# The second edge gather of a graph and expert kernel: waits and signals by quad, a lead of 11 pairs

## The chip, the cores and the metric

The kernel runs on one core of one Trainium2 chip. Its engines are TensorE (PE), VectorE (DVE), ScalarE (ACT), GpSimd (POOL) and SyncE (SP), each with a queue of its own. They meet through semaphores only. The metric is the device time of one execution in microseconds, the median of several runs.

## The reference

A graph step is followed by a layer of experts. The change touches the graph step: for each of 100,000 edges, sorted by target node, the normalised row of one end is scaled by the edge's weight and summed into the other end's row; the sums are multiplied by W and added to x.

```python
x.shape == (6250, 256); src, dst, edge_weight: 100000
h    = _layernorm(x) @ W.T
msgs = edge_weight[:, None] * h[dst]
x    = x + segment_sum(msgs, src, 6250)
...
x    = x + experts(_layernorm(x))    # 16 experts, the two best of each row, then a norm
```

The kernel sums the rows before it multiplies by W, which gives the same.

## The kernel before

The 6250 nodes are 49 windows of 128. Edges are first sorted by window into tiles of 128 edges. A first part of them (four tiles a window) is gathered and summed early, in straight code, while the sorting still runs. The rest, up to 640 tiles here, is the second gather. It runs after the tables are ready, in loops, and it is the only stage that the change touches.

Its unit is the pair, two tiles of 128 edges. Two pairs are a quad. 16 pairs are one turn of the ring `hbuf` (PR = 16), and there are 20 turns. For a quad of a window PE runs four matmuls of 128 x 128 by 128 x 256 (fp32, each two rows in the profile), which add into the window's bank: the weights are `picks`, a matrix for each tile that says which edge goes to which node, with the edge's weight in it, and the moving rows are those gathered in `hbuf`. The last quad of a window may hold edges of the next one too, so it is read twice: once as the window's closing quad, and again as the first loop quad of the next window. `picks` is 256 wide for that reason, and its two halves serve even and odd windows.

Five queues take part, in an order written out by hand.

- POOL (`gather_gpsimd`, L464) issues two indirect DMAs for a pair (L473). Ahead of a pair it waits for `used`, the count of pairs that PE has finished: pair p may be issued when all but the last AHEAD = 6 pairs before and with it are used. The row numbers lie in `ix`, copied there by DVE in halves (`number`, L422). POOL waits for `ix_set` at each half turn.
- DVE (`gather_vector`, L481) makes the picks of a pair with two instructions (L498), into one of two buffers. So it waits until the pair before the last one is used. It adds to `pick_ready`. Three times in the stage it also ranks the experts for windows that are done (`choose`).
- SP (`gather_sync`, L444) joins the two: for each pair it waits for `pick_ready` and for the gathered rows (`xn_gathered`), then adds one to `pair_in` (L461).
- PE (`gather_tensor`, L550) waits for `pair_in` ahead of each pair of a quad (L554), and its last matmul of each pair adds one to `used` (L591). The closing quad adds nothing to `used`; its last matmul adds one to `closed`. Behind the closing quad stand, for earlier windows, `turn` (two transposes of the sums of the window before, L565) and `project` (the product with W, the gate's columns and the addition of x for the window before that, L572 to L574). The next window starts with a matmul that puts the first sums into its bank (L588).
- ACT (`gather_scalar`, L612) copies the bank to `agg` when `closed` says so (L634), copies the transposed sums (L616), and takes x and its squares (L621 to L628).

When all windows are through, the experts follow. They need every row, so the end of the second gather delays all that comes after.

## Time and profile before

| | |
|---|---|
| median of 3 runs | 2196.22 us (2194.57 to 2212.91) |
| profiled execution | 2194.18 us, span 2192.4 us |
| PE busy | 1521.2 us, 69% |
| POOL busy | 1206.6 us, 55% |
| DVE busy | 976.2 us, 45% |
| ACT busy | 642.5 us, 29% |
| gathers of the second stage (L473) | 640, first at 604.7 us, last at 1593.2 us |
| granted TensorE clock, mean over the span | 0.831 of full speed |

Busy time is the time in which an engine ran instructions that work on data; waits, register work and the issue of DMAs by queues don't count. "Idle before" a group is the time that the engine stood still ahead of its instructions, and the name behind the arrow is what ended it: an instruction of another engine, a DMA, "issue" where the profile shows no reason, or "remote" where a semaphore moved and the profile can't name who moved it. The granted clock is 0.5 or 1.0 at each moment, 1.2 or 2.4 GHz. The ends of matmuls in the rows are modelled, the times of semaphores are not.

### The profile page before, as it was taken

Reading aid. Unit: us, or ns where it says so; the run is one execution under the profiler, and the core shown is the slowest. Engines: PE = TensorE matmul, PEld = TensorE weight load, DVE = VectorE, ACT = ScalarE, POOL = GpSimd, SP = SyncE. Lnnn points to the kernel's source line nnn. Section 1 sums busy time; section 2 is a strip of 40 time slices with the busy share of each in tenths; the row PEclk is TensorE's granted clock in tenths of the full one; section 3 lists DMA queues with packets and bytes.
Section 4 is the critical chain, followed back from the end, with each engine's and each line's share of the span. In section 5 each row is a group of like instructions: output and inputs, shape, how many; then the busy total and the mean of one; then the engine's idle time right before and its main releaser. Section 6 shows DMA issues by size and latency. Waiting matters only on the chain. (4 is left out here: it accounts for less than half of the span.)

```text
span 2192.4 us, 33976 instructions
## 1 busy us (share of the span) xinstructions
PE 1521.2 (69%) x7875; PEld 1191.4 (54%) x7876; DVE 976.2 (45%) x2548; ACT 642.5 (29%) x1788; POOL 1206.6 (55%) x1170
## 2 busy tenths in 40 slices
PE   6165977775655766666666577766436999998975
PEld 4164766553334544444444344544325998897864
DVE  6997898863322222222222422223164333333348
ACT  5661266641000111110110111011053444443455
POOL 0025658776666666666666656665532555554435
PEclk9596679886678878887888788887659999999988
DMA  5122322223633223222222222222363223225356
GB/s 169 51 71 61 90 60 69 64 74 98 211 105 92 83 83 87 87 86 82 85 86 86 82 77 85 88 85 78 76 155 135 69 71 104 86 81 180 104 166 230
DMA packets 121466, 215.63 MB, mean 98 GB/s; under 512 B 21000, under 2 KB 82755, under 8 KB 121280
## 3 DMA queue, kind: packets, MB, share of 16 engines
q0 software_dynamic: 52864, 140.45, 21.9%
q1 hardware_dynamic: 53664, 56.14, 7.8%
q10 hardware_dynamic: 14880, 18.35, 2.6%
q8 instruction: 26, 0.43, 0.1%
q14 instruction: 32, 0.26, 0.0%
HBM read 172.32 MB, written 42.54 MB: 98 GB/s over the span
## 5 line engine op out<-in xcount | busy, mean ns | idle before, releaser
L473 POOL DMA_INDIRECT hbuf<-xn_rows,ix x640 | 618.3, 966 | 375.1 <-issue 173.2
L556 PE MATMUL bank<-hbuf,picks 128*128 x1640 | 536.2, 473 | 340.6 <-SPq L461 193.7
L556 PEld LDWEIGHTS bank<-hbuf,picks 128*128 128x128 f32 x1640 | 351.2, 232 | 519.0 <-issue 470.9
L498 DVE TENSOR_SCALAR picks<-iota_two,marks 128x256 f32<-128x256 f32 x640 | 247.9, 434 | 726.3 <-remote 420.6
L744 POOL DMA_INDIRECT fbuf<-xn_rows,first_tables x196 | 235.8, 1203 | 122.6 <-PE bank L1269 54.7
L634 ACT ACTIVATE agg<-bank 128x256 f32<-128x256 f32 x49 | 18.8, 383 | 763.3 <-remote 579.3
L1853 PE MATMUL bank<-rowsT,w_sb 128*128 128x128 f32 x1744 | 215.8, 277 | 18.9 <-issue 18.9
L1853 PEld LDWEIGHTS bank<-rowsT,w_sb 128*128 128x128 f32 x1744 | 211.6, 193 | 31.1 <-issue 26.6
L1789 POOL DMA_INDIRECT expert_out<-y_sb,to_i x112 | 111.1, 992 | 189.9 <-DVE y_sb L1898 185.4
L1863 PE MATMUL bank<-w_sb,hT 128*128 128x256 f32 x872 | 207.7, 381 | 0.6 <-ACT hT L1811 0.4
L1287 PE MATMUL bank<-work 128*128 128x192 bf16 x1568 | 161.0, 261 | 62.7 <-DVE work L1075 50.3
L1269 PE MATMUL bank<-fbuf,x 128*128 128x256 f32 x392 | 153.1, 506 | 53.0 <-DMA fbuf<-xn_rows,first_tables 40.6
L1287 PEld LDWEIGHTS bank<-work 128*128 128x128 bf16 x1568 | 143.4, 102 | 85.3 <-issue 80.9
L1811 ACT ACTIVATE hT<-bank,b_cols 128x128 f32<-128x128 f32 x436 | 138.5, 365 | 161.2 <-PE bank L1853 150.8
L1863 PEld LDWEIGHTS bank<-w_sb,hT 128*128 128x128 f32 x872 | 157.0, 190 | 18.9 <-ACT hT L1811 1.6
L733 POOL DMA_INDIRECT edge_groups<-recs,dest_i x56 | 79.1, 1413 | 156.9 <-DVE recs L1082 140.3
L1779 POOL DMA_INDIRECT xt<-xn_rows,from_i x116 | 112.6, 970 | 68.6 <-issue 36.7
L1269 PEld LDWEIGHTS bank<-fbuf,x 128*128 128x128 f32 x392 | 81.0, 241 | 85.1 <-issue 55.8
L1898 DVE TENSOR_TENSOR y_sb<-bank,b_b 128x256 f32 x109 | 46.3, 425 | 163.4 <-PE bank L1863 157.3
L1103 DVE TENSOR_SCALAR x<-iota_two,first_tables 128x128 f32<-128x128 f32 x196 | 64.8, 364 | 107.3 <-PE bank L1269 48.6
L1075 DVE TENSOR_TENSOR work<-work,tables 128x768 bf16<-128x768 bf16 (+2 forms) x176 | 95.5, 599 | 5.6
L1059 DVE TENSOR_TENSOR work<-iota_rows,low_i 128x512 bf16<-128x512 bf16 (+2 forms) x136 | 95.1, 749 | 0.2 <-DVE tables L1154 0.2
(294 smaller groups left out, 1721.7 us busy)
## 6 DMA issues: line engine op xcount, KB each, us to landing
w_sb<-in_L_ffn_w_dram ACTq DMA_DIRECT2D x28, 512.0 KB
hbuf<-xn_rows,ix POOLq DMA_INDIRECT x640
first_sums<-x SPq DMA_DIRECT2D x49, 128.0 KB
first_sums_back<-first_sums SPq DMA_DIRECT2D x7, 896.0 KB
xn_rows<-xn SPq DMA_DIRECT2D x7, 896.0 KB, 4.6
x<-in_x_dram SPq DMA_DIRECT2D x6, 896.0 KB
ya<-expert_out SPq DMA_DIRECT2D x5, 896.0 KB, 5.6
yb<-expert_out SPq DMA_DIRECT2D x5, 896.0 KB, 7.5
```

The source lines that it names most:

```text
L473: pool.indirect_dma_start(hbuf[:, 1 + j, k, :], None, xn_dram, bass.IndirectOffsetOnAxis(ap=ix[:, 2 * j + k:2 * j + k + 1], axis=0)).then_ ...
L498: s = v.tensor_scalar(picks[:, j % 2, k, :], iota_two[:], marks[:, 0, 2 * j + k:2 * j + k + 1], marks[:, 1, 2 * j + k:2 * j + k + 1], ALU. ...
L556: m = nc.tensor.matmul(bk[q][:, 0:D], picks[:, j, k, q * P:(q + 1) * P], hbuf[:, ds(place + j, 1), k, :].rearrange("p s d -> p (s d)"), st ...
L744: pool.indirect_dma_start(fbuf[:, s % RH, :], None, xn_dram, bass.IndirectOffsetOnAxis(ap=fdst_i[:, s:s + 1], axis=0)).then_inc(xn_gathere ...
L1075: s = v.tensor_tensor(fields[n % RM][:, h0:h1, :, :, :], colhot[n % RJ][:, h0:h1, None, :, :].to_broadcast(shape), pieces[:, e0 + h0:e0 + ...
L1269: nc.tensor.matmul(bk[w % 2][:, 0:D], fpicks[:, used % RK, :], fbuf[:, used % RH, :], start=t == 0, stop=t == FT - 1).then_inc(first_used, 1)
L1287: s = nc.tensor.matmul(sums_at[c % 2][h][:, 0:2 * PIECES * SP_], rowhot[n % RP][:, k // 2, h * P:(h + 1) * P, k % 2], fields[n % RM][:, k ...
L1779: pool.indirect_dma_start(xt[:, k, :], None, xn2_dram, bass.IndirectOffsetOnAxis(ap=from_i[:, k:k + 1], axis=0)).then_inc(xt_in[k], 16)
L1789: pool.indirect_dma_start(y_dram, bass.IndirectOffsetOnAxis(ap=to_i[:, k:k + 1], axis=0), y_sb[:, k % 2, :], None).then_inc(y_sent[k], 16)
L1811: act.activation(hT[:, f, :], bk[f][:, 0:P], ACT.Relu, bias=b1_cols[:, ds(e * FB + f, 1)]).then_inc(hT_ready, 1)
L1853: m = nc.tensor.matmul(bk[f][:, 0:P], w1_sb[:, q, b, f * P:(f + 1) * P], rowsT[:, b, :], start=b == 0, stop=b == NB - 1)
L1863: m = nc.tensor.matmul(bk[5][:, 0:D], hT[:, f, :], w2_sb[:, q, f, :], start=f == 0, stop=f == FB - 1)
```

## The change

PE waits once for a quad, for its second pair, and adds two to `used` at its last matmul, in place of one at the end of each pair. POOL's lead AHEAD goes from 6 to 11 pairs. The numbers are copied in quarters of 8 in place of halves of 16, at other points of DVE's turn. In a window of PE, `turn` and `project` stand ahead of the closing quad, behind the loop. DVE's waits for `used`, and SP's and ACT's waits, stay as they are.

```diff
--- before.py
+++ after.py
@@ -386,7 +386,7 @@
 
 
         PR = GR // 2
-        AHEAD = 6
+        AHEAD = 11
         hbuf = sb("hbuf", [P, 1 + PR, 2, D], fp32)
         ix = sb("ix", [P, GR], i32)
         marks = sb("marks", [P, 2, GR], fp32)
@@ -417,10 +417,11 @@
         mean2_set = sem("mean2_set")
         squared2 = sem("squared2")
 
-        HALF = GR // 2
+        PART = PR // 4
+        NUMBERS = 2 * PART
 
         def number(v, i, h):
-            v.tensor_copy(ix[:, h * HALF:(h + 1) * HALF], dst_i[:, ds(i * GR + h * HALF, HALF)]).then_inc(ix_set, 1)
+            v.tensor_copy(ix[:, h * NUMBERS:(h + 1) * NUMBERS], dst_i[:, ds(i * GR + h * NUMBERS, NUMBERS)]).then_inc(ix_set, 1)
 
         assert PR == RH
 
@@ -465,8 +466,8 @@
             pool.wait_ge(tables_ready, FBLK + 1)
             def body(i, ahead):
                 for j in range(PR):
-                    if j % (PR // 2) == 0:
-                        pool.wait_ge(ix_set, i * 2 + (j // (PR // 2) + 1))
+                    if j % PART == 0:
+                        pool.wait_ge(ix_set, i * 4 + (j // PART + 1))
                     await_turn(pool, used, i, PR, j + 1 + PR - ahead)
                     pool.sem_inc(pool_steps, 1)
                     for k in range(2):
@@ -500,12 +501,11 @@
                     s.then_inc(pick_ready, 1)
 
                     if j == 2 and not isinstance(i, int):
-
                         await_turn(dve, pair_in, i, PR, 0)
-                        number(v, i, 1)
-                    if j == PR // 2 + 2:
-                        await_turn(dve, pair_in, i, PR, PR // 2)
-                        number(v, i + 1, 0)
+                        number(v, i, 3)
+                    if j > PART and j % PART == 2:
+                        await_turn(dve, pair_in, i, PR, j - 2)
+                        number(v, i + 1, j // PART - 1)
 
             def choose(w0, w1):
                 n, ws = w1 - w0, slice(w0, w1)
@@ -550,8 +550,8 @@
         def gather_tensor(pe):
             def quad(s, q):
                 place = s & (PR - 1)
+                pe.wait_ge(pair_in, s + 1)
                 for j in range(2):
-                    pe.wait_ge(pair_in, s + j)
                     for k in range(2):
                         m = nc.tensor.matmul(bk[q][:, 0:D], picks[:, j, k, q * P:(q + 1) * P],
                                              hbuf[:, ds(place + j, 1), k, :].rearrange("p s d -> p (s d)"),
@@ -588,15 +588,16 @@
                 nc.tensor.matmul(bk[q][:, 0:D], ident[:], first_sums[:, ds(w, 1), :].rearrange("p w d -> p (w d)"), start=True, stop=False, skip_group_check=True)
                 with pe.Fori(first, end, 2) as s:
                     for m in quad(s, q):
-                        m.then_inc(used, 1)
-
-                for m in quad(end, q):
-                    pass
-                m.then_inc(closed, 1)
+                        pass
+                    m.then_inc(used, 2)
+
                 if not isinstance(w, int) or w >= 1:
                     turn(w - 1, 1 - q)
                 if not isinstance(w, int) or w >= 2:
                     project(w - 2, q)
+                for m in quad(end, q):
+                    pass
+                m.then_inc(closed, 1)
 
             pe.wait_ge(tables_ready, FBLK + TBLK)
             pe.wait_ge(first_summed, NW)
@@ -1192,8 +1193,8 @@
                     dve.wait_ge(recs_turned, FBLK + b + 1)
                     table(b, turned_1(b), min(P, TT - b * P), dst_i, row_f, wgt_f, tables_ready)
                     picks_to(SORT_TILES + 20 + b)
-                number(v, 0, 0)
-                number(v, 0, 1)
+                for h in range(4):
+                    number(v, 0, h)
                 picks_to(FTILES)
                 gather_vector(dve)
```

PE's queue in the loop of one window, before. `pair_in` is SP's count of pairs ready; a matmul here is one tile, L589 is the loop's end:

```order
L556 REGISTER_ALU [waits pair_in]
L556 ISA
L556 MATMUL bank<-hbuf,picks 128x256
L556 ISA
L556 MATMUL bank<-hbuf,picks 128x256
L554 REGISTER_ALU
L556 ISA [waits pair_in]
L556 MATMUL bank<-hbuf,picks 128x256
L556 ISA
L556 MATMUL bank<-hbuf,picks 128x256
L589 REGISTER_ALU
L589 COMPARE_AND_BRANCH
```


The same place in the changed kernel:

```order
L556 REGISTER_ALU [waits pair_in]
L556 ISA
L556 MATMUL bank<-hbuf,picks 128x256
L556 ISA
L556 MATMUL bank<-hbuf,picks 128x256
L556 ISA
L556 MATMUL bank<-hbuf,picks 128x256
L556 ISA
L556 MATMUL bank<-hbuf,picks 128x256
L589 REGISTER_ALU
L589 COMPARE_AND_BRANCH
```


The second wait is gone, and the register steps stand together behind the first.

PE's queue behind that loop, before: the closing quad and then the transposes of the window before (L565).

```order
L556 REGISTER_ALU [waits pair_in]
L556 ISA
L556 MATMUL bank<-hbuf,picks 128x256
L556 ISA
L556 MATMUL bank<-hbuf,picks 128x256
L554 REGISTER_ALU
L556 ISA [waits pair_in]
L556 MATMUL bank<-hbuf,picks 128x256
L556 ISA
L556 MATMUL bank<-hbuf,picks 128x256
L565 MATMUL bank<-ident,agg 128x128 [waits aggT_ready,agg_ready]
L565 MATMUL bank<-ident,agg 128x128
```


And changed (L572 to L574 are the projection; the closing quad begins with the wait for `pair_in`):

```order
L589 COMPARE_AND_BRANCH
L565 MATMUL bank<-ident,agg 128x128 [waits aggT_ready,agg_ready]
L565 MATMUL bank<-ident,agg 128x128
L572 MATMUL bank<-wT,aggT 128x272 [waits aggT_ready]
L572 MATMUL bank<-wT,aggT 128x272
L573 MATMUL bank<-x,ident 128x16
L574 MATMUL bank<-x,ident 128x256
L553 REGISTER_ALU
L556 REGISTER_ALU [waits pair_in]
L556 ISA
L556 MATMUL bank<-hbuf,picks 128x256
L556 ISA
```


The transposes and the projection moved from behind the closing quad's four matmuls to the place between the loop and the closing quad's wait.

DVE's queue at the copy of numbers in the middle of a turn, before:

```order
L25 REGISTER_ALU [waits used]
L498 TENSOR_SCALAR picks<-iota_two,marks 128x256 [waits pick_ready]
L498 TENSOR_SCALAR picks<-iota_two,marks 128x256
L423 ISA [waits pair_in]
L423 COPY ix<-tables 128x16
```


And at the first of the three such places after the change:

```order
L25 REGISTER_ALU [waits used]
L499 TENSOR_SCALAR picks<-iota_two,marks 128x256 [waits pick_ready]
L499 TENSOR_SCALAR picks<-iota_two,marks 128x256
L424 ISA [waits pair_in]
L424 COPY ix<-tables 128x8
```


The copy is half as wide, and it stands at pairs 2, 6, 10 and 14 of a turn in place of 2 and 10.

## Rows read from the trace of the kernel before

**Rows 1.** The page: the span, the busy shares, and the matmuls of the line.

```profile
span 2192.4 us, 33976 instructions
...
PE 1521.2 (69%) x7875; PEld 1191.4 (54%) x7876; DVE 976.2 (45%) x2548; ACT 642.5 (29%) x1788; POOL 1206.6 (55%) x1170
...
L556 PE MATMUL bank<-hbuf,picks 128*128 x1640 | 536.2, 473 | 340.6 <-SPq L461 193.7
```

**Rows 2.** The gather's own line: its instructions, and what POOL sat idle for.

```profile
L473 POOL DMA_INDIRECT hbuf<-xn_rows,ix x640: 947/953/2118, 604.7 to 1593.2; - x160
...
  remote: 96.6, 33
  PE bank L556: 92.6, 56
  DVE ix L423: 12.7, 1
```

**Rows 3.** Waits of SyncE's queue, 620 to 1590 us: total, times, longest.

```profile
SPq L461 <- DVE picks L498: 569.1, 166, 26.7
...
SPq L461 <- DMA hbuf<-xn_rows,ix: 18.3, 12, 2.3
```

**Rows 4.** Timeline of POOL, 880 to 990: start, length, idle before it.

```profile
945.22 0.95 POOL L473 DMA_INDIRECT hbuf<-xn_rows,ix  x1 [0.30 <-issue]
949.44 1.01 POOL L473 DMA_INDIRECT hbuf<-xn_rows,ix  x1 [3.27 <-remote]
950.76 0.95 POOL L473 DMA_INDIRECT hbuf<-xn_rows,ix  x1 [0.30 <-issue]
...
963.33 0.95 POOL L473 DMA_INDIRECT hbuf<-xn_rows,ix  x1 [0.30 <-issue]
967.70 1.01 POOL L473 DMA_INDIRECT hbuf<-xn_rows,ix  x1 [3.42 <-PE bank L556]
```

**Rows 5.** Timeline of PE, 952 to 976: closing quad, transposes, last projection.

```profile
956.39 2.10 PE L556 MATMUL bank<-hbuf,picks 128*128 x8 [0.40 <-issue]
958.32 0.38 PE L565 MATMUL bank<-ident,agg 128*128 128x128 f32 x2
...
959.60 0.68 PE L574 MATMUL bank<-x,ident 128*128 x2
```

**Rows 6.** Timelines of ACT, PE's weight loads and DVE, the same stretch.

```profile
966.09 0.38 ACT L634 ACTIVATE agg<-bank 128x256 f32<-128x256 f32 x1 [15.25 <-remote]
...
968.32 0.73 PEld L556 LDWEIGHTS bank<-hbuf,picks 128*128 128x128 f32 x4 [0.81 <-issue]
...
956.03 0.16 DVE L423 COPY ix<-tables 128x16 int32 x1
...
967.15 0.74 DVE L498 TENSOR_SCALAR picks<-iota_two,marks 128x256 f32<-128x256 f32 x2 [9.99 <-PE bank L556]
...
969.70 0.76 DVE L498 TENSOR_SCALAR picks<-iota_two,marks 128x256 f32<-128x256 f32 x2 [0.49 <-PE bank L556]
```

**Rows 7.** Timelines of PE and DVE, 936 to 952: a window's first quad.

```profile
942.77 1.89 PE L556 MATMUL bank<-hbuf,picks 128*128 x8
...
948.90 1.38 DVE L498 TENSOR_SCALAR picks<-iota_two,marks 128x256 f32<-128x256 f32 x4 [9.51 <-remote]
```

**Rows 8.** Timeline of POOL, 1018 to 1034, a window of four loop quads.

```profile
1032.01 1.01 POOL L473 DMA_INDIRECT hbuf<-xn_rows,ix  x1 [5.63 <-PE bank L556]
```

**Rows 9.** Timelines: four picks; a quad; two quads at the lower clock.

```profile
1003.38 1.38 DVE L498 TENSOR_SCALAR picks<-iota_two,marks 128x256 f32<-128x256 f32 x4 [9.05 <-PE bank L556]
...
914.78 1.99 PE L556 MATMUL bank<-hbuf,picks 128*128 x8 [0.39 <-SPq L461]
...
907.88 6.52 PE L556 MATMUL bank<-hbuf,picks 128*128 x16 [2.24 <-SPq L461]
```

**Rows 10.** Stretches: busy time (count) by engine, granted clock, DMA share, GB/s.

```profile
610.00:1600.00 990.00, 644.66 (x2190) 444.02 (x2191) 267.15 (x710) 107.49 (x417) 614.23 (x636) 0.81 0.30 85
906.00:913.00 7.00, 5.12 (x12) 3.96 (x13) 2.93 (x9) 2.19 (x9) 4.43 (x5) 0.55 0.23 66
```


## The prediction

> **What bounds the kernel now.** I read the page's busy shares first. No engine is near full: TensorE (PE) 69%, GpSimd (POOL) 55%, VectorE (DVE) 45% [rows 1]. The change touches the second gather alone, so the question is what sets the length of that stage. It comes from the gather's line: POOL issues 640 gathers between 604.7 and 1593.2 us, that is 988.5 us, or 20.2 us for each of the 49 windows [rows 2]. One gather costs POOL 0.95 us and the 0.30 us of issue behind it, 1.257 us from start to start (950.76 to 963.33 is ten of them [rows 4]). 640 of them are 804.5 us, or 16.4 us a window. The rest, some 184 us, is POOL waiting. The same line says for what: 96.6 us in 33 waits for an event whose sender the trace can't name, 92.6 us in 56 waits for PE's matmuls, and 12.7 us in one wait for DVE's numbers [rows 2]. All of the first two are waits on "used". So POOL is not the bound by itself; it stands at its lead of six pairs and waits for PE to free slots.
>
> Is PE then waiting for data? The wait list of the queue that joins picks and landed rows says no: it waited 569.1 us for DVE's picks and 18.3 us for the gathers [rows 3]. The rows are there; the loop of DVE (picks) and PE (matmuls, "used") is what is late.
>
> Where in a window it is late is seen in the timelines. POOL's waits come once a window and look alike: 3.27 and 3.42 us idle in two windows that follow each other [rows 4], 2.93 in the mean of the 33 [rows 2], where 0.30 is normal. In the boundary at 956 us PE finishes the closing quad at 956.39 + 2.10 = 958.5, yet ScalarE (ACT), which waits for nothing but "closed", copies the sums at 966.09, 7.6 us later [rows 5, 6]. In the window before, the quad that opens a window ends at 942.77 + 1.89 = 944.7, and DVE's next picks, which wait for its "used", start at 948.90 [rows 7]. So PE's signals come several us behind the matmuls that carry them. And in each of these windows they come about 3.5 to 3.8 us after POOL's last gather started: 945.22 and 948.90, 963.33 and 967.15 [rows 4, 6, 7], whatever PE did. I read it thus: around a boundary PE's signals are held until POOL has run out of lead and its last gathers have landed. The trace doesn't show the cause, and I don't claim one.
>
> **The change, part by part.**
>
> *Lead 11 instead of 6.* If the held signals are let go when POOL stops, a longer lead doesn't remove the stop. POOL then still issues one window's tiles (16.4 us) and pauses once: 3.27 - 0.30 = 2.97 us. 48 pauses, one for each boundary, are 142 us. What a longer lead does take away is every wait beyond this one. All waits are 96.6 + 92.6 + 12.7 = 201.9 us in 90 times; less 90 x 0.30 of normal issue, 174.9; less 142, 33 us. To these belong the 12.7 us in which DVE ranked experts and had not copied the numbers [rows 2], and the part above 3 us of stops such as the 5.63 us at the end of a window of four loop quads [rows 8]. Five pairs more are 5 x 2 x 1.257 = 12.6 us of cover, about as long as the longest. So this part gives 33 us; its bounds are 0 (other work takes the time) and 175 us (no pause is left at all).
>
> *Numbers in quarters.* Two copies of 0.16 us [rows 6] for each turn of 16 pairs become four smaller ones. Over 20 turns that is at most 40 x 0.16 = 6.4 us more on DVE, which is busy 45% of the span [rows 1] and waits for PE in every window. Nothing, then. It is what lets POOL be 11 ahead. Quarter k of the next turn is copied at DVE's pair 4k + 6, just as "used" admits POOL to it. If DVE ranks at that moment POOL waits, as once now.
>
> *One wait and one signal a quad.* This is the part with a price. Now DVE makes the picks of a pair while PE multiplies the pair before: two pairs' picks start at 967.15, the next two's at 969.70, 2.55 us later [rows 6]. After the change "used" moves only at a quad's end, and PE starts only when all four tiles are there, so the two take turns. A loop quad then costs picks 1.38 us [rows 9], the hop to PE 0.43 (967.15 + 0.74 to the weight load at 968.32 [rows 6]), matmuls 1.99 [rows 9], and a hop back, which I estimate at 0.25 from the first hop less what the joining queue adds: 4.05 us at the full clock, against 2.55 now. At the half clock 16 matmul rows take 6.52 [rows 9], so 3.3 for a quad, and the loop quad costs 5.4. POOL needs 4 x 1.257 = 5.03 us for the same quad. At the full clock the loss lies under POOL's issue; at the half clock it doesn't.
>
> *Turn and project ahead of closing.* They run from 958.32 to 959.60 + 0.68 = 960.28, 1.96 us [rows 5]. Now they stand between the closing quad and the next window's first quad, whose "used" DVE and POOL wait for. Moved, they run while DVE makes the closing quad's picks (1.38 + 0.43 = 1.81), so about 1.8 us leave the chain per window. A boundary, from one "used" to the next, costs 1.96 + 1.99 + 0.43 (first sums) + 1.99 + 0.25 = 6.6 us at the full clock, and with all PE work doubled 13.0 less the hop's share, 12.6, at the half clock.
>
> *The chain's sum.* The 1640 matmul rows of the line are 8 a quad, 205 quads [rows 1]; 49 of them close a window, 156 are loop quads, 3.2 a window, one of which sits in the boundary. 2.2 x 4.05 + 6.6 = 15.5 us at the full clock, 2.2 x 5.4 + 12.6 = 24.5 at the half clock. The granted clock of the stage is 0.81 [rows 10], which is 38% of the time at 1.2 GHz: 18.9 us. POOL with its one pause is 16.4 + 2.97 = 19.4. The present window is 20.2. So the chain just fits under POOL, the pause stays, and the gain is the 33 us above.
>
> One rule of the notes is weighed here. Each of the 156 loop quads carries two signals now and one afterwards, and what the rows show of signals is a lateness of several us [rows 5 to 7]. The Trainium skill (TensorE: Matmul & The Clock Gate, The cost: per-tile semaphore tail) says that increments at the end of matmuls serialize, about 26 ns each, and that a single one on the last is sound. By that 156 signals fewer would be 4 us, an estimate from that page. No row here shows such a cost, and the sum above goes without it.
>
> Sum: 2194.2 (the profiled execution, span 2192.4) - 33 = 2161. The median of the runs, 2196.2, stands 2 us above it. I predict **2160 us**.
>
> **Rivals.**
>
> *The pauses go too* (chance 0.20). If signals are let go after some us of their own, and POOL's stop only looks like the cause, a lead of 27.7 us (11 pairs) outlasts the hold. For it: no row names the event that lets the signals go, and with six pairs of lead a hold of 8 us and POOL's stop always fall together, so the trace can't part them. Against it: the sameness of the stops [rows 4]. The time would be 2194 - 175 = 2019, some us more for the last windows: 2025.
>
> *The turn-taking loop becomes the bound* (0.22), the slower side. PE will have a gap of over 2 us in every quad. Behind the stop that ends at 907 us the clock granted for 7 us was 0.55 [rows 10]. If the gaps keep it low, the chain passes the present 20.2 us once more than (20.2 - 15.5) / 9.0 = 52% of the time is at 1.2 GHz, a granted clock of 0.74 or less. At 0.66 it is 21.6 us, 1.4 x 49 = 69 us longer: 2265. Held signals inside the loop would have the same effect, as every one then stops DVE at once. The Trainium skill (same page, Part 1: The HAM clock gate) says that the throttled state is the default and activity releases it, which speaks for this rival. The trace agrees in direction only.
>
> *Nothing measurable* (0.16): the chain of DVE and PE takes what the lead gives, and the stage stays at 20.2 us a window; 2195.
>
> **How the numbers follow.** My case has 0.42, with its own range 2125 to 2195. A measurement of this kernel can tell about 1% from no change, 22 us. Faster by more than that (under 2174): 0.20 and about 0.3 of my 0.42, together 0.50. Within 1%: 0.12 of mine and most of the 0.16, 0.26. Slower: 0.24. The range 2040 to 2240 leaves out half of the first rival and the upper half of the second, about 2 in 10.
>
> **What would show it.** Right: 640 gathers over some 955 us; POOL's idle stretches of about 3.3 us still once a window, none of 5 to 13 us; DVE's picks in blocks of four (1.38 us), 4 to 5.4 us apart; turn and project ahead of the closing quad's matmuls; granted clock near 0.8. The first rival: POOL's idle is nearly all issue, and the line lasts about 810 us. The second: a granted clock under 0.74, POOL waiting for PE in nearly every quad, over 200 us in total. My forecast is wrong at its root if held signals don't follow POOL's stop, that is if ACT's copy comes at another distance than 3 to 4 us from POOL's last gather.

## The result, and the profile after

The changed kernel takes 2218.4 us in the median of 12 runs (2207.0 to 2227.8). The kernel before, run on the same chip, takes 2199.9 us (2189.9 to 2212.9, 12 runs). The ratio is 1.0081, 95% interval 1.0057 to 1.0105: 0.8% slower, 18 us. I had forecast 2160 us and "faster" as the likeliest case. The time lies inside the range, but the direction is wrong.

These rows of the page after answer [rows 1], and the rows of the gather's and the picks' own lines answer [rows 2]. In the last two, the numbers behind "x640" are shortest, median and longest in ns, then the first and the last start in us.

```profile
span 2226.0 us, 33938 instructions
...
L474 POOL DMA_INDIRECT hbuf<-xn_rows,ix x640 | 623.1, 974 | 383.4 <-issue 179.6
L556 PE MATMUL bank<-hbuf,picks 128*128 x1640 | 529.9, 479 | 348.5 <-SPq L462 310.8
L499 DVE TENSOR_SCALAR picks<-iota_two,marks 128x256 f32<-128x256 f32 x640 | 229.8, 413 | 762.7 <-PE bank L556 480.6
```

```profile
L474 POOL DMA_INDIRECT hbuf<-xn_rows,ix x640: 951/957/2112, 614.6 to 1615.2; - x160
...
  PE bank L556: 118.3, 60
  remote: 69.7, 25
  DVE ix L424: 15.7, 6
...
L499 DVE TENSOR_SCALAR picks<-iota_two,marks x640: 395/408/641, 614.2 to 1635.6; 128x256 f32<-128x256 f32 x160
```

POOL waits as long as before: 118.3 + 69.7 + 15.7 = 203.7 us, against 201.9 in [rows 2]. So the lead of 11 pairs has taken no waiting away. PE's wait for the joining queue has grown from 193.7 us [rows 1] to 310.8, and that queue waits for DVE's picks. This is the same line of picks in the kernel before:

```profile
L498 DVE TENSOR_SCALAR picks<-iota_two,marks x640: 394/411/645, 604.1 to 1607.4; 128x256 f32<-128x256 f32 x160
```

From the first pick to the last that is 1003.3 us, and 1635.6 - 614.2 = 1021.4 after the change. The two profiled spans are 33.6 us apart: 10.1 of them lie before the first pick, 18.1 between the first and the last, and 5.4 after it. The change hardly touches what stands outside the stage. The 18.1 agrees with the 18 us of the medians, but two single executions can't prove so small a difference, as executions of one kernel differ by some 20 us among themselves. Of the 18.1, 12.1 lie between POOL's first and last gather (1000.6 us here, 988.5 in [rows 2]). Another 6.2 lie behind the last gather: the last pick comes 1635.6 - 1615.2 = 20.4 us after it, and 14.2 in the kernel before.

Timelines of POOL, PE, DVE and ACT of the changed kernel, 912 to 936 us (start, length, engine and line, idle time before it and who ended it), show one window. Dots stand for lines left out:

```profile
916.52 1.03 POOL L474 DMA_INDIRECT hbuf<-xn_rows,ix  x1 [2.73 <-remote]
...
930.91 0.96 POOL L474 DMA_INDIRECT hbuf<-xn_rows,ix  x1 [0.30 <-issue]
934.78 0.95 POOL L474 DMA_INDIRECT hbuf<-xn_rows,ix  x1 [2.91 <-remote]
...
923.07 2.78 PE L556 MATMUL bank<-hbuf,picks 128*128 x8 [1.91 <-SPq L462]
...
927.86 0.68 PE L574 MATMUL bank<-x,ident 128*128 x2
928.38 1.89 PE L556 MATMUL bank<-hbuf,picks 128*128 x8
...
921.41 1.38 DVE L499 TENSOR_SCALAR picks<-iota_two,marks 128x256 f32<-128x256 f32 x4 [3.98 <-PE bank L556]
...
934.14 1.38 DVE L499 TENSOR_SCALAR picks<-iota_two,marks 128x256 f32<-128x256 f32 x4 [6.05 <-remote]
...
934.08 0.38 ACT L635 ACTIVATE agg<-bank 128x256 f32<-128x256 f32 x1 [15.79 <-remote]
```

The order that the prediction described is there. Picks come in blocks of four. DVE stands still while PE multiplies, and PE while DVE picks. `project` (L574) runs ahead of the closing quad (928.38). The closing quad ends at 930.3 and ACT's copy starts at 934.08, 3.17 us after POOL's last gather started. POOL's pause is still there once a window (2.73, 2.91 us). This window takes 18.26 us from pause to pause, about what POOL needs for three quads and its pause (3 x 5.03 + 2.97 = 18.06). Others take longer, and the experiments are about those.

### The profile page after: what moved, and what is told of

Read it like the earlier page. It is cut to its first block and busy times, and to the rows that moved or that the text cites. A ratio compares the mean times of both kernels' runs of the same rounds, so it can differ in the third digit from the quotient of the medians.

```text
span 2226.0 us, 33938 instructions
## 1 busy us (share of the span) xinstructions
PE 1544.6 (69%) x7875; PEld 1237.2 (56%) x7876; DVE 959.0 (43%) x2590; ACT 638.9 (29%) x1788; POOL 1212.8 (54%) x1170
## 5 line engine op out<-in xcount | busy, mean ns | idle before, releaser
L556 PE MATMUL bank<-hbuf,picks 128*128 x1640 | 529.9, 479 | 348.5 <-SPq L462 310.8
L556 PEld LDWEIGHTS bank<-hbuf,picks 128*128 128x128 f32 x1640 | 371.7, 237 | 488.6 <-issue 427.0
L499 DVE TENSOR_SCALAR picks<-iota_two,marks 128x256 f32<-128x256 f32 x640 | 229.8, 413 | 762.7 <-PE bank L556 480.6
L635 ACT ACTIVATE agg<-bank 128x256 f32<-128x256 f32 x49 | 18.8, 384 | 900.6 <-remote 699.6
L1270 PE MATMUL bank<-fbuf,x 128*128 128x256 f32 x392 | 161.4, 529 | 52.6 <-DMA fbuf<-xn_rows,first_tables 40.4
L1864 PEld LDWEIGHTS bank<-w_sb,hT 128*128 128x128 f32 x872 | 157.0, 191 | 20.4 <-ACT hT L1812 3.3
```

The lines of the kernel that those rows point to most:

```text
L499: s = v.tensor_scalar(picks[:, j % 2, k, :], iota_two[:], marks[:, 0, 2 * j + k:2 * j + k + 1], marks[:, 1, 2 * j + k:2 * j + k + 1], ALU. ...
L556: m = nc.tensor.matmul(bk[q][:, 0:D], picks[:, j, k, q * P:(q + 1) * P], hbuf[:, ds(place + j, 1), k, :].rearrange("p s d -> p (s d)"), st ...
L1270: nc.tensor.matmul(bk[w % 2][:, 0:D], fpicks[:, used % RK, :], fbuf[:, used % RH, :], start=t == 0, stop=t == FT - 1).then_inc(first_used, 1)
L1864: m = nc.tensor.matmul(bk[5][:, 0:D], hT[:, f, :], w2_sb[:, q, f, :], start=f == 0, stop=f == FB - 1)
```

## The experiments

The sums over windows in this table are worked out from each trace. "Window of 3" and "of 4" are medians over windows with three (39) and four (9) loop quads, from a window's first pick to the next one's. "Inside" is the mean from one quad's picks to the next one's within a window, "boundary" the same over the quad that closes one window and opens the next. "Late" counts the windows whose `closed` moved over 2 us after the closing quad's last weight load, among those where both events are in the trace. All times are us. Each trace is one execution.

| kernel | ratio to before | first to last pick | window of 3 | of 4 | inside | boundary | late |
|---|---|---|---|---|---|---|---|
| before | 1 | 1003.3 | 19.0 | 23.1 | 3.48 | 12.88 | 41 of 45 |
| after | 1.0081 | 1021.4 | 18.7 | 24.6 | 5.20 | 9.31 | 37 of 47 |
| e1, lead and quarters | 1.0042 | 988.8 | 18.8 | 22.8 | 3.33 | 12.92 | 42 of 43 |
| h3, quarters | 1.0004 | 987.7 | 18.6 | 23.0 | 3.36 | 12.84 | 40 of 44 |
| e3, turn ahead | 0.9993 | 980.1 | 17.8 | 24.5 | 3.50 | 12.35 | 45 of 48 |
| e4, lead and turn ahead | 1.0016 | 984.0 | 18.3 | 22.8 | 3.40 | 12.67 | 42 of 46 |
| e2, quad | 1.0335 | 1053.8 | 20.0 | 26.0 | 5.18 | 10.03 | 8 of 36 |
| f1, quad and turn ahead | 1.0034 | 1016.8 | 18.5 | 25.2 | 5.27 | 9.05 | 38 of 46 |
| f2, quad and lead | 1.0329 | 1061.6 | 20.4 | 26.0 | 5.14 | 10.30 | 21 of 40 |
| f3, after with two signals | 1.0091 | 1027.8 | 19.5 | 24.9 | 4.18 | 11.78 | 38 of 47 |
| g3, lead 3 | about 1.067 | 1111.3 | 20.7 | 26.5 | 4.95 | 11.76 | 1 of 45 |
| f4, before without gathers | | 618.7 | 11.2 | 13.6 | 2.71 | 6.65 | 1 of 48 |
| h1, quad without gathers | | 978.0 | 18.0 | 23.5 | 4.81 | 9.31 | 1 of 48 |
| h2, after without gathers | | 851.0 | 15.3 | 21.0 | 4.64 | 7.05 | 1 of 48 |

Kernels whose names begin with the same letter ran on one chip together, with their own runs of the kernel before (medians 2172.7, 2202.7, 2164.4 and 2175.5 us for e, f, g and h). So ratios can be compared across letters, and bare times only within one; e and h share a chip. The chips' own times differ by up to 1.8%, and differences of that size between the traces of different letters say nothing.

### The change in its parts

The first four kernels each do a part of the change alone, or leave one out.

**e1, lead 11 and quarters on the kernel before.**

```diff
-        AHEAD = 6
+        AHEAD = 11
```

with the numbers in quarters, as in the change's diff.

> The kernel before with the lead of 11 pairs and the numbers in quarters, nothing else. Theory A (PE's held signals come only when POOL has stopped, so a longer lead moves the stop and doesn't remove it): within 0.5% of before, POOL still stops once a window for about 3 us. Theory B (a longer lead pays for itself, and the turn-taking loop hid that): 30 us or more faster.

Measured: 2182.2 us against 2172.7, ratio 1.0042 (1.0016 to 1.0068). The 33 us of the prediction aren't there; the part even costs a little. The waits in its gather's line show why:

```profile
L474 POOL DMA_INDIRECT hbuf<-xn_rows,ix x640: 951/957/2111, 605.8 to 1575.6; - x160
...
  remote: 90.7, 31
  PE bank L557: 90.3, 69
  DVE ix L424: 6.7, 12
```

POOL still waits 90.7 + 90.3 + 6.7 = 187.7 us. The nearest kernel is h3 (below), with quarters but a lead of 6, on the same chip: there POOL waits 180.4 us for the same three (85.5, 89.0 and 5.9), and the line of picks takes 987.7 us where e1 takes 988.8. POOL stops for over 1 us 49 times in e1 and 51 times in h3, mostly for some 3 us, about once a window. At each such stop the lead is spent. So what comes on top (a slow window, a ranking) is added in full, and no stock is left from quick windows. A longer lead also moves where POOL's line ends: the last pick comes 1593.9 - 1575.6 = 18.3 us after the last gather starts, and 14.2 us in the kernel before (1607.4 - 1593.2).

A longer lead can even make a wait longer. These are POOL and DVE in the second window, first in e1 and then in h3:

```profile
647.33 0.96 POOL L474 DMA_INDIRECT hbuf<-xn_rows,ix  x1 [0.31 <-issue]
653.56 0.96 POOL L474 DMA_INDIRECT hbuf<-xn_rows,ix  x1 [5.27 <-remote]
...
652.96 1.38 DVE L499 TENSOR_SCALAR picks<-iota_two,marks 128x256 f32<-128x256 f32 x4 [27.64 <-remote]
```

```profile
628.78 0.95 POOL L474 DMA_INDIRECT hbuf<-xn_rows,ix  x1 [0.30 <-issue]
633.44 0.96 POOL L474 DMA_INDIRECT hbuf<-xn_rows,ix  x1 [3.71 <-issue]
...
632.85 1.38 DVE L499 TENSOR_SCALAR picks<-iota_two,marks 128x256 f32<-128x256 f32 x4 [14.00 <-remote]
```

POOL had issued from the stage's start to 647.33 and to 628.78 without a stop, and in both cases DVE got PE's signals only after POOL stopped. With the lead of 11 it stood still for 27.64 us in place of 14.00. The second window takes 34.4 to 40.8 us in each of the six kernels here with a lead of 11, and 21.8 to 24.9 in all ten with a lead of 6. POOL's last turn has a lead of 16 pairs in every kernel. Coming from 6 to 16, the last window but one, the 48th, takes 34.4 us in h3 (11.2 without gathers, in f4); coming from 11, the 47th and 48th take 27.0 and 16.7 in e1, where h3 has 19.5 and 34.4. So e1 gets back at the end most of what it loses at the start, and the two stages are equal.

**e2, one wait and one signal a quad, on the kernel before.**

```diff
+                pe.wait_ge(pair_in, s + 1)
                 for j in range(2):
-                    pe.wait_ge(pair_in, s + j)
...
-                        m.then_inc(used, 1)
+                        pass
+                    m.then_inc(used, 2)
```

> The kernel before with one wait and one signal a quad, nothing else. Theory A (the turn-taking of DVE and PE is what cost the changed kernel its time): 20 to 60 us slower than before, a loop quad every 4 to 5.7 us where it was 2.5, more of POOL's waits. Theory B (the loop's length is hidden under POOL's issue and pause): within 0.5%.

Measured: 2248.0 us, ratio 1.0335 (1.0291 to 1.0379), by that ratio 73 us slower, and more than theory A's 20 to 60. This part alone costs four times what the whole change costs. Timelines of POOL, PE, DVE and ACT, 786 to 809:

```profile
786.47 1.00 POOL L473 DMA_INDIRECT hbuf<-xn_rows,ix  x1 [4.90 <-PE bank L556]
...
797.17 1.02 POOL L473 DMA_INDIRECT hbuf<-xn_rows,ix  x1 [0.87 <-PE bank L556]
...
806.88 1.03 POOL L473 DMA_INDIRECT hbuf<-xn_rows,ix  x1 [4.90 <-PE bank L556]
...
798.29 3.77 PE L556 MATMUL bank<-hbuf,picks 128*128 x8 [1.91 <-issue]
...
804.20 1.89 PE L556 MATMUL bank<-hbuf,picks 128*128 x8
...
796.63 1.38 DVE L498 TENSOR_SCALAR picks<-iota_two,marks 128x256 f32<-128x256 f32 x4 [4.30 <-PE bank L556]
...
806.33 0.73 DVE L498 TENSOR_SCALAR picks<-iota_two,marks 128x256 f32<-128x256 f32 x2 [8.32 <-PE bank L556]
...
802.26 0.38 ACT L635 ACTIVATE agg<-bank 128x256 f32<-128x256 f32 x1 [16.61 <-PE bank L556]
```

Nothing is late here: the closing quad ends at 802.06 and ACT copies at 802.26. But the closing quad runs at the lower clock, 3.77 us. From its picks to the next picks pass 806.33 - 796.63 = 9.70 us, and POOL, which may issue only four tiles in that time, stops for 4.90 in place of 3. This window of three loop quads takes 806.88 - 786.47 = 20.41 us, by the chain and not by POOL. It is no exception: POOL stops for more than 4 us 27 times in e2 and 7 times in h3, whose time is that of the kernel before.

**e3, turn and project ahead of the closing quad, on the kernel before.**

```diff
-                for m in quad(end, q):
-                    pass
-                m.then_inc(closed, 1)
                 if not isinstance(w, int) or w >= 1:
                     turn(w - 1, 1 - q)
                 if not isinstance(w, int) or w >= 2:
                     project(w - 2, q)
+                for m in quad(end, q):
+                    pass
+                m.then_inc(closed, 1)
```

> The kernel before with turn and project ahead of the closing quad, nothing else. Theory A (the boundary's work lies under the hold of the signals in windows of three loop quads, and on the path only in windows of four): 0 to 20 us faster. Theory B (every window gains the 1.96 us of turn and project): 49 x 1.96, about 90 us faster.

Measured: 2174.6 us, ratio 0.9993 (0.9970 to 1.0017). Alone, it changes nothing that can be measured. That fits a kernel in which POOL and its pause are the bound.

**e4, the changed kernel with a wait and a signal for each pair again** (so lead, quarters and turn ahead without the quad part).

> The changed kernel with a wait and a signal for each pair again, so lead and turn ahead alone. Theory A (turn-taking cost the time, the other two parts are worth something): faster than before by 10 to 40 us, and than the changed kernel by 30 to 60. Theory B (the other parts cost the time): as slow as the changed kernel, about 2218 us.

Measured: 2178.7 us, ratio 1.0016 (0.9988 to 1.0044), no change, where theory A had a gain of 10 to 40 us. Against the changed kernel's 1.0081 it is better beyond both intervals. So what the change loses, it loses by the quad part. Yet that part costs 3.35% alone and less than 1% in company, and the next two say which company.

### Which part makes up for the quad part

**f1, quad and turn ahead; f2, quad and lead 11.** Their diffs are those of e2 and e3, and of e2 and e1.

> The kernel before with two of the parts: one wait and one signal a quad, and turn and project ahead of the closing quad; lead still six pairs. The quad part alone made 1.0335, all parts together 1.008. Theory T (the turn ahead of closing is what gives it back, since PE then works in the time in which it waits for the closing quad's picks): 1.008 to 1.013. Theory L (the long lead gives it back, since slow windows are covered by rows landed in fast ones): 1.03 or more here. Both half: near 1.02.

> The kernel before with two of the parts: one wait and one signal a quad, and lead 11 with numbers in quarters; turn and project stay behind the closing quad. Theory T: 1.03. Theory L: 1.008 to 1.013. Both half: near 1.02.

Measured: f1 2211.7 us against 2202.7, ratio 1.0034 (0.9990 to 1.0078); f2 2266.0, ratio 1.0329 (1.0266 to 1.0392). f1 comes out even better than theory T's 1.008 to 1.013. It is the order at the boundary that makes up for it, and the lead does nothing. The weight loads of f1 around one boundary, 945 to 953, show how:

```profile
945.58 3.04 PEld L556 LDWEIGHTS bank<-hbuf,picks 128*128 128x128 f32 x8 [2.70 <-issue]
948.64 0.36 PEld L565 LDWEIGHTS bank<-ident,agg 128*128 128x128 f32 x2
948.97 0.76 PEld L572 LDWEIGHTS bank<-wT,aggT 128*128 128x128 f32 x4
...
950.92 1.59 PEld L556 LDWEIGHTS bank<-hbuf,picks 128*128 128x128 f32 x8 [0.51 <-issue]
```

The last loop quad (945.58) loads in 3.04 us, at the lower clock. The transposes and the projection follow at once, and the closing quad (950.92) loads in 1.59 us, at 2.4 GHz. The eight loads of a closing quad are 0.39 us apart at the lower clock and 0.20 to 0.22 at 2.4 GHz. By this spacing the closing quad runs at 2.4 GHz from end to end in 11 of 49 windows of e2 and in 46 of 49 of f1. So the reorder does two things: it fills a gap in which PE waits for picks, and behind that work PE meets the closing quad at the higher clock. No run parts the two. The boundary takes 10.30 us in f2 and 9.05 in f1, on one chip.

**f3, the changed kernel with two signals a quad** and one wait.

```diff
-                        pass
-                    m.then_inc(used, 2)
+                        m.then_inc(used, 1)
```

> The changed kernel, still with one wait a quad, but 'used' moves after each pair again, twice a quad. Theory A (what costs is that VectorE's picks and TensorE's matmuls take turns): VectorE can make the next quad's first two picks while the second pair is multiplied, about 0.7 us a quad less, so half or more of the loss goes: 1.001 to 1.005. If the wait for all four tiles is the whole loss: 1.008, as the changed kernel. Block pick-to-pick inside a window about 4.5 us instead of 5.2 in the mean.

Measured: 2222.3 us, ratio 1.0091 (1.0059 to 1.0124). I expected 1.001 to 1.005 from the earlier picks, and missed. Quads inside a window do come a microsecond sooner (4.18 in place of 5.20), but the boundary comes later (11.78 in place of 9.31), with `closed` 5.39 us behind the loads in the mean, and 4.30 in the changed kernel. The time doesn't move. Against e4, f3 differs by the wait for all four tiles alone, and has 1.0091 where e4 has 1.0016. So that wait is where the loss is, and the count of signals isn't.

### The chain alone

**f4, the kernel before without gathers.** POOL gathers the first 16 pairs only, and PE goes on to multiply these old rows, so that the output is another.

```diff
             def body(i, ahead):
+                if not isinstance(i, int):
+                    return
...
-                    sp.wait_ge(xn_gathered[j], i * 32 + (16 * first_turns(j) + 32))
+                    if isinstance(i, int):
+                        sp.wait_ge(xn_gathered[j], i * 32 + (16 * first_turns(j) + 32))
```

> The kernel before without its gathers: GpSimd gathers only the first turn of 16 pairs and nobody waits for landings after it, so the rows multiplied are old ones. It shows the chain of VectorE and TensorE alone. Theory A (TensorE's signals are late because gathers are in flight, and are let go when they have landed): 'closed' comes within 1 us of the closing quad's matmuls, and a window takes 9 to 12 us, so the stage is 450 to 600 us. Theory B (TensorE's signals are late by something of its own, the boundary's work or its throttle): 'closed' stays 5 to 8 us late in most windows and a window keeps 15 us or more, stage above 700 us.

Measured, in one execution: 1795.9 us, 407 less. In the timelines of PE and ACT, 898 to 926, nothing is late:

```profile
911.35 1.99 PE L555 MATMUL bank<-hbuf,picks 128*128 x8 [0.46 <-SPq L462]
...
913.53 0.38 ACT L633 ACTIVATE agg<-bank 128x256 f32<-128x256 f32 x1 [9.89 <-PE bank L555]
```

The closing quad ends at 913.34 and ACT copies at 913.53. It is so in 47 of 48 windows (mean 0.6 us behind the loads, and 5.6 in the kernel before). The one late window is the first, in which the 32 gathers of the first turn are still being issued. The late signals of [rows 5 to 7] need gathers in flight, as theory A said. A window of three takes 11.2 us, and the line of picks 618.7, a little over theory A's 600.

**h1, e2 without gathers, and h2, the changed kernel without gathers** (the same edit).

> The kernel before with one wait and one signal a quad (nothing else of the change), and without its gathers after the first turn (the rows multiplied are old ones). It measures the taking of turns by itself. From rows: a loop quad 4.05 us at the full clock, 5.4 at the half clock; a boundary 8.4 at the full clock (picks 1.38, hop 0.43, closing 1.99, turn and project 1.96, sums and opening 2.42, hop 0.25), some 14 at the half. Theory K (taking turns lowers the clock by itself, as TensorE idles half of the time): granted clock in the stage under 0.8, windows of three loop quads over 19 us, stage over 950 us. Theory G (the low clock comes with the gathers, from the holds and waits): clock 0.9 or more, windows of three 16 to 17 us, of four 20 to 21, stage 800 to 840 us.

> The changed kernel without its gathers after the first turn (the rows multiplied are old ones). The prediction's chain at the full clock: 6.6 us a boundary and 4.05 a loop quad, so 14.7 us for a window of three, 18.8 for one of four, stage some 760 us (the kernel before without gathers: 11.2, 13.6 and 618). Theory K: clock under 0.8, windows of three over 18 us. Theory G: clock 0.9 or more, windows as the sum says, within 0.5 us.

Measured, one execution each: 2168.1 us for h1, and 2024.5 for h2. The rows of 700 to 1150 us from the three kernels f4, h1 and h2, in that order (busy time and count by engine, then the granted clock, the DMA share and GB/s):

```profile
700.00:1150.00 450.00, 389.53 (x1712) 299.94 (x1711) 192.08 (x535) 87.01 (x340) 0.00 (x0) 0.98 0.00 0
```

```profile
700.00:1150.00 450.00, 307.51 (x1059) 228.78 (x1060) 106.87 (x328) 53.52 (x207) 0.00 (x0) 0.80 0.00 0
```

```profile
700.00:1150.00 450.00, 327.35 (x1261) 243.50 (x1262) 126.17 (x406) 61.09 (x251) 0.00 (x0) 0.89 0.00 0
```

The clock falls from 0.98 to 0.80 with nothing changed but the taking of turns, and no gather in flight. So the taking of turns lowers it, as theory K said. K's numbers for h1 come out in part: the stage was to be over 950 us and is 978.0, the clock sits at K's bound of 0.8, but windows of three take 18.0 us and not over 19 (theory G had 16 to 17). h1's boundaries take 9.31 us in the mean, nearer to the 8.4 expected at the full clock than to the 14 at the half. With `turn` and `project` ahead the clock is 0.89, which lies between the two theories. Some of DVE's rows in h2 give the chain's prices at the higher clock:

```profile
903.24 0.73 DVE L498 TENSOR_SCALAR picks<-iota_two,marks 128x256 f32<-128x256 f32 x2 [5.10 <-PE bank L555]
...
907.11 1.38 DVE L498 TENSOR_SCALAR picks<-iota_two,marks 128x256 f32<-128x256 f32 x4 [1.96 <-PE bank L555]
910.99 0.73 DVE L498 TENSOR_SCALAR picks<-iota_two,marks 128x256 f32<-128x256 f32 x2 [2.50 <-PE bank L555]
...
917.92 1.38 DVE L498 TENSOR_SCALAR picks<-iota_two,marks 128x256 f32<-128x256 f32 x4 [5.48 <-PE bank L555]
```

At the higher clock a loop quad of the changed kernel costs 910.99 - 907.11 = 3.88 us (predicted 4.05), the boundary 917.92 - 910.99 = 6.93 (predicted 6.6), and the window of three 917.92 - 903.24 = 14.68 (predicted 14.7). Two small errors cancel in the last. The medians are higher, 15.3 and 21.0 for the windows of three and four, and the stage takes 851.0 us where the expectation had 760, since part of it runs at the lower clock. The prediction's sum at a clock of 0.89 is 15.5 + 0.22 x 9.0 = 17.5 us a window, and 851.0 / 49 = 17.4 is measured.

### What starts the late signals

**g1, the projection cut to one matmul.** It issues four matmuls of 8 rows, not the ten that the expectation says, and now 2 rows.

```diff
-                for b in range(NB):
-                    nc.tensor.matmul(bk[4 + q][:, 0:D + EX], aggT[q][:, b, :], wT[:, b, :], start=b == 0, stop=False, ...)
...
+                s = nc.tensor.matmul(bk[4 + q][:, 0:D + EX], aggT[q][:, 0, :], wT[:, 0, :], start=True, stop=True, ...)
```

> The kernel before with the projection at each boundary cut from 10 matmuls to one (the sum it computes is left out but for one part, so the output is another). It asks what makes TensorE's signals late at a boundary. If it is the long run of TensorE's work there (closing, turn, project, opening back to back): 'closed' is late over 2 us in fewer than half of the windows (41 of 45 read in the kernel before) and the stage is 60 us shorter or more. If it is something else at the boundary (loading the window's bounds, leaving the loop): still late in 35 or more, stage within 20 us.

**g2, a load more in each loop quad.**

```diff
                 with pe.Fori(first, end, 2) as s:
+                    pe.value_load(quad_i[0:1, ds(w, 1)], min_val=1, max_val=TT // 2)
```

> The kernel before with one load more of a window bound into a TensorE register in every loop quad (its value isn't used). If such a load is what starts a hold of TensorE's signals while gathers are in flight: each quad's signals come late, GpSimd stops in nearly every quad (150 stops instead of 56), and the stage is 200 us longer or more. If not: the load costs its 0.75 us a quad behind waits, the stage stays within 30 us.

Measured, one execution each beside 2164.4 for the kernel before: g1 2162.8 us (its output is another), `closed` late in 39 of 43 windows; g2 2179.2 us, late in 39 of 45, with 54 stops of POOL where 56 were before. Neither shortening the projection nor adding a load changes how often it happens.

**g3, a lead of three pairs.** The edit is AHEAD = 3.

> The kernel before with a lead of three pairs instead of six. Theory A (a hold ends when GpSimd's last gathers have landed, whatever the lead; each window is its gathers' issue and one stop of 3 us): windows of three loop quads still 18 to 19 us in the median, stage within 25 us, but 'closed' only 3 to 4.5 us late in the mean, as GpSimd comes to its stop sooner (5.6 in the kernel before). Theory C (a hold lasts 5 to 8 us of its own): still 5.6 late, each stop 3 us longer, stage 100 to 150 us longer.

Measured: 2308.4 us. Both theories miss. `closed` comes 1.3 us behind the loads in the median, hardly late at all, and still the kernel takes 144 us more than the one before on that chip. Timelines of POOL, DVE and ACT, 909 to 919:

```profile
911.69 0.95 POOL L473 DMA_INDIRECT hbuf<-xn_rows,ix  x1 [0.30 <-issue]
918.80 1.01 POOL L473 DMA_INDIRECT hbuf<-xn_rows,ix  x1 [6.16 <-PE bank L556]
...
918.25 0.74 DVE L498 TENSOR_SCALAR picks<-iota_two,marks 128x256 f32<-128x256 f32 x2 [8.01 <-PE bank L556]
914.89 0.38 ACT L634 ACTIVATE agg<-bank 128x256 f32<-128x256 f32 x1 [16.66 <-PE bank L565]
```

POOL reaches its limit at 911.69, before the closing quad is done. PE's signals then come in time, but the whole boundary, 6 us of it, lies open in POOL's stop. With a lead of three the boundary is no longer covered; with six and with eleven, late signals leave a gap of 3 us in each window in its place. g3 is a single execution, and its granted clock is also lower, 0.77 over the span against 0.84 for the kernel before beside it, so its loss may not be the lead's reach alone.

**g4, every other gather left out** after the first turn, with SP's counts of landed gathers halved to match.

```diff
-                    for k in range(2):
+                    for k in range(2 if isinstance(i, int) and i == 0 else 1):
```

> The kernel before with every other gather of the second gather left out after the first turn (half the rows multiplied are old ones). GpSimd then issues 336 gathers, 422 us, and has time to spare; the chain of VectorE and TensorE alone took 12.6 us a window. Theory A: with GpSimd standing at its lead most of the time few gathers are in flight at a boundary, 'closed' is late by 1 to 3 us in the mean, a window takes 12.5 to 15 us. If any gather in flight holds the signals for long: 5 us late in the mean still, a window 16 us or more.

Measured, in one execution: 1857.3 us. `closed` is 1.4 us behind the loads in the mean and late in 2 of 46 windows, and a window takes 666.8 / 49 = 13.6 us. As theory A expects, fewer gathers in flight make the signals less late.

**h3, quarters alone**, lead 6.

> The kernel before with the numbers copied in quarters and nothing else; lead still six pairs. Lead 11 with quarters made 1.0042. If the copies are what costs: 1.003 to 1.005 here. If the longer lead is (more rows landed and taken late): 0.999 to 1.001. The prediction had nothing for the copies, since VectorE waits for TensorE in every window.

Measured: 2175.4 us against 2175.5, ratio 1.0004 (0.9975 to 1.0032). The copies cost nothing that can be measured. The small loss of e1 then belongs to the longer lead, if it is one: the intervals of e1 and h3 overlap, and e4, which has the lead too, shows 1.0016. No kernel here beats the one before by more than its interval.

## Why the prediction was wrong

**Where it was right.** The pause of some 3 us at POOL once a window stays with lead 11 (rows of after; e1). The late signals come with the gathers and are gone without them (f4). In the changed kernel they end some 3 us after POOL's last gather starts: 31 of 37 late windows lie 2.7 to 3.6 us behind it. "Whatever PE did" was too wide, though, and rested on two windows: in the kernel before, `closed` lies in that band in only 12 of 41 late windows, and in most others it comes before POOL stops or early in the stop. The rival in which the pauses go is thereby out. Quarters cost nothing (h3). The chain's sum was good for a kernel without gathers (17.5 and 17.4 us a window at h2's clock). With gathers it is too low: at the changed kernel's clock of 0.79 the same sum gives 15.5 + 0.42 x 9.0 = 19.3, and 990.5 / 48 = 20.6 is measured.

**The lead's 33 us: the term is 0, or a small loss** (e1: 9 us slower, 3 to 15). I took all waiting beyond one pause a window as something that a longer lead absorbs. A lead absorbs a delay only if it is there when the delay comes. Here POOL stops about once a window because the lead is spent, whatever its length, so the delay is added behind it. The step that failed is "what a longer lead does take away is every wait beyond this one", although the sentences before it had POOL run into its limit in every window. They also imply what I didn't price: if signals are held until POOL stops, a longer lead holds them longer where it begins (second window, 14.00 and 27.64 us). I misread the 12.7 us too. It isn't time in which DVE ranked experts; its ranking instructions start at 1247.5, 1493.5 and 1611.0 (L521). These are DVE and POOL of the kernel before:

```profile
1565.93 1.38 DVE L498 TENSOR_SCALAR picks<-iota_two,marks 128x256 f32<-128x256 f32 x4 [26.11 <-remote]
...
1574.35 0.95 POOL L473 DMA_INDIRECT hbuf<-xn_rows,ix  x1 [12.66 <-DVE ix L423]
```

DVE stood still for 26.11 us for PE's late signals, and so came late to the copy of numbers for which POOL waited.

**"So the chain just fits under POOL": the quad part costs 73 us alone (e2), and 7 with the reorder (f1, whose interval runs from 2 us faster to 17 slower).** This second step failed too, and it is the one that makes the change slower. I compared two means, 18.9 us for the chain and 19.4 for POOL. But with the lead spent at each boundary a quick window leaves nothing for a slow one. If so, each window takes the longer of the two for itself. The traces allow a rough test: for each of the 48 windows, the longer of the chain's time in the kernel without gathers and of POOL's 5.03 us for each loop quad and 2.97 for the pause. With h1's windows, for the quad part alone, that gives 966.9 us, and with f4's 923.6: 43 us. Measured are 1016.7 us in e2 and 955.9 in h3 on the same chip, 61 apart, and 73 by the ratio. So the rule explains more than half of e2's loss and not all.

For the whole change the rule shows less than it seems to. With h2's windows it gives 945.5 us, 22 more than with f4's, and the measured windows of the two profiled executions are also 990.5 - 968.6 = 22 apart. But 13.1 of the rule's 22 us lie in the first two windows, in which h2 and f4 still gather and the longer lead holds the signals; 8.5 lie in two windows in which DVE ranks experts. In 43 of the 48 windows the rule has no change, while the measured ones go from 14 us shorter to 9 us longer. That the two numbers agree is in part luck. All these sums lie some 32 to 50 us under the measured ones: gathers in flight make the chain itself longer, and this sum doesn't have that. What is shown for the whole change is where the loss is, in the wait for all four tiles (e4 and f3), and not how it comes about in each window.

**The clock.** I took the granted clock of the kernel before, 0.81, for the chain after, and set a fall to 0.74 as a rival. In the changed kernel it is 0.79, in e2 0.74, the very point at which that rival was to begin, and e2 is slower as it said. These are the rows of the stage, e2 first, then after, where [rows 10] has 0.81:

```profile
620.00:1640.00 1020.00, 670.77 (x2170) 490.91 (x2169) 242.31 (x704) 107.98 (x417) 608.26 (x627) 0.74 0.28 80
```

```profile
620.00:1630.00 1010.00, 652.58 (x2202) 477.38 (x2203) 247.53 (x751) 102.06 (x417) 618.87 (x636) 0.79 0.29 83
```

That it is the taking of turns that lowers the clock, and not the gathers, is shown by h1 and f4 (0.80 and 0.98 with none in flight). The rival had the right mechanism and came true for the quad part; what kept the whole change from it is the reorder (f1), which I had priced without the clock. The Trainium skill (TensorE: Matmul & The Clock Gate, Part 1: The HAM clock gate) says that the throttled state is the default and that activity releases it; by that rule new gaps between matmuls cost more than their own length, and here the trace agrees (0.98 in f4, 0.80 in h1).

**Turn and project ahead of closing.** I gave it 1.8 us a window, 86 us over 48, as something that shortens the chain, and let it lie under POOL. Measured are 3.35 - 0.34 = 3.0%, 66 us, where the chain is the bound (e2 to f1), and nothing where POOL is (e3). So I had the condition right and the size within a third. Part of the 66 us is the closing quad's higher clock, which my 1.8 us didn't have.

**Fewer signals.** The Trainium skill (TensorE: Matmul & The Clock Gate, The cost: per-tile semaphore tail) would give some 4 us for 156 signals fewer, an estimate from that page. No run here shows it: with both signals the changed kernel has 1.0091, with one 1.0081, and the intervals overlap.

**What stays open.** Why PE's signals are late while gathers are in flight isn't settled. It isn't the length of the projection (g1) nor, as far as one more load shows, the loading of bounds (g2). It isn't the loading of instructions either: only 7 DMA packets of instructions fall into the stage of the kernel before, in which 41 windows were late. It came less often where PE's quads were spread out by waits (8 of 36 windows in e2), and nearly always where PE ran them close together (45 of 48 in e3); that is a correlation and not a test. Open too are the last 30 us of e2's loss, and whether the longer lead costs 0.4% or nothing. No run gave DVE more than two buffers of picks, which might keep the overlap with one wait a quad.

## What to carry to other kernels

Ask whether a lead or a buffer ever fills again: where each round ends in a stop at its limit, more lead was worth nothing here and made one early wait twice as long. There a comparison of two chains by their means can miss what single rounds cost. Waiting for a whole group in place of its parts, between two engines that feed each other, took their overlap away, and with it TensorE's clock (0.98 to 0.80). So price such a part at the lower clock and by itself. Work moved into the gap in front of a matmul group was worth 3.0% where that gap was new, and nothing where it wasn't.

## What the runs showed of the hardware

- With indirect gathers in flight, TensorE's semaphore updates at the ends of windows came 5.6 us behind the last weight load in the mean (before), 1.4 with half the gathers (g4), and 0.6 without them (f4). In the changed kernel 31 of the 37 late ones came 2.7 to 3.6 us after the start of a gather that was POOL's last before a stop, in the kernel before 12 of 41.
- At the start of the stage the wait grew with POOL's unbroken run of gathers: 14.00 us after 24 gathers (h3), 27.64 after 34 (e1).
- In the same stretches register instructions of TensorE's queue, 46 ns long otherwise, took about 700 ns: some 170 of them in the stage of the kernel before, some 70 after, none in f4 without gathers. SyncE's queue had 19 between 600 and 800 ns before and 16 after.
- A loop in which TensorE and VectorE take turns had a granted clock of 0.80 with no DMA running, where the same work with one pair of overlap had 0.98.
